# Where the image attention's short operations stand among the maxima of a two-layer cross-attention kernel

## The reference

```
# layer 0
q = x Wq;  out = softmax(q k_text) v_text + softmax(q k_img) v_img
x = out Wo + bo + x
# layer 1
probs_t = softmax(q k_t * scale);  text_out = probs_t v_t
attn_scores = q k_ip * scale                     # 4 image columns a head
qsem = l2norm(probs_t @ text);  ip_n = l2norm(ip)
fused = attn_scores + 0.5 * (qsem . ip_n)
probs_ip = softmax(fused) * spatial_mask
out = (text_out + probs_ip v_ip) W_out + b_out + x
```

## Time and profile before

| | |
|---|---|
| median of 3 runs | 2523.54 us (2521.98 to 2524.99) |
| the profiled execution's own time | 2525.83 us |
| its span | 2524.0 us |
| granted TensorE clock, mean | 0.996 |
| PE busy | 2444.6 us, 97% |
| DVE busy | 1642.0 us, 65% |
| ACT busy | 1228.2 us, 49% |
| POOL busy | 774.2 us, 31% |
| chain that ended last | PE 71%, DVE 17%, POOL 4% |

### The profile page before, as it was taken

How to read it: one execution, slowest core, us unless ns; L and a number is a source line. 1 busy time by engine, 2 the same in 40 slices (tenths; PEclk the granted TensorE clock), 3 DMA queues, 4 the chain that set the end, 5 groups by cost and what they waited for, 6 DMA issues and landing times.

```text
span 2524.0 us, 64056 instructions
## 1 busy us (share of the span) xinstructions
PE 2444.6 (97%) x26372; PEld 2117.5 (84%) x26372; DVE 1642.0 (65%) x3313; ACT 1228.2 (49%) x2251; POOL 774.2 (31%) x1030
## 2 busy tenths in 40 slices
PE   7899999999999999999999999999999999999998
PEld 6788888888888888888888888888888888888877
DVE  4456667666667666667656677566677666677665
ACT  3355444455444455444554454554454554444543
POOL 3133233233233232233232233332332332332322
PEclk9999999999999999999999999999999999999999
DMA  8865446674556754557655466645566655566620
GB/s 216 139 100 88 93 88 98 106 116 75 88 90 96 117 90 85 89 92 113 104 81 97 80 106 104 108 76 91 97 97 105 98 82 91 88 97 103 95 28 18
DMA packets 371689, 241.44 MB, mean 96 GB/s; under 512 B 131947, under 2 KB 365243, under 8 KB 371388
## 3 DMA queue, kind: packets, MB, share of 16 engines
q1 hardware_dynamic: 371398, 237.35, 56.6%
HBM read 171.35 MB, written 64.59 MB: 93 GB/s over the span
## 4 chain that ended last, share of the span: by engine, by line
PE 71%; DVE 17%; POOL 4%; DMA 2%; SPq 2%; issue 2%; ACT 1%; DVEq 0%; POOLq 0%; ACTq 0%
PE ST L832 7%; PE R L898 5%; PE R L763 5%; PE PN L871 5%; PE R L708 4%; DVE m L1090 4%; POOL w L1468 4%; PE R L776 4%; PE R L777 4%; PE R L709 4%; PE R L956 3%; DVE m L1094 3%; PE PN L916 3%; DVE w L992 3%; PE R L779 3%; PE R L711 3%
## 5 line engine op out<-in xcount | busy, mean ns | idle before, releaser
L1468 POOL TENSOR_TENSOR w<-w 128x448 f32<-128x448 f32 (+1 forms) x256 | 331.2, 1294 | 376.8 <-DVE w L989 358.0
L992 DVE SCALAR_TENSOR_TENSOR w<-p,pr 128x1344 f32<-128x1344 f32 x160 | 295.9, 1850 | 164.6 <-ACT pr L1352 151.0
L1324 ACT ACTIVATE p<-ST 128x1344 f32<-128x1344 f32 x260 | 335.5, 1290 | 99.0 <-PE ST L835 94.0
L989 DVE TENSOR_TENSOR rem<-R,kst 128x298 f32<-128x298 f32 (+2 forms) x180 | 89.4, 497 | 426.5 <-ACT kst L1207 426.3
L898 PE MATMUL R<-pr,Gh 128*128 128x448 f32 (+1 forms) x960 | 366.3, 382 | 0.0
L989 DVE TENSOR_TENSOR w<-R,w 128x448 f32<-128x448 f32 (+1 forms) x480 | 281.7, 620 | 69.4 <-PE R L903 59.2
L1400 POOL TENSOR_TENSOR kst<-rem,kst 128x298 bf16<-128x298 f32 (+2 forms) x180 | 148.0, 822 | 558.1 <-ACT kst L1207 305.2
L776 PE MATMUL R<-wvh,ch 128*128 128x320 f32 (+3 forms) x896 | 302.9, 338 | 0.0
L777 PE MATMUL R<-wvh,cl 128*128 128x320 f32 (+3 forms) x896 | 277.4, 310 | 0.0
L832 PE MATMUL ST<-Qs,Ks 100*128 100x112 bf16 (+1 forms) x3520 | 228.9, 214 | 8.2 <-ACT p L1324 2.7
L832 PEld LDWEIGHTS ST<-Qs,Ks 100*128 100x128 bf16 (+1 forms) x3520 | 187.9, 98 | 46.7 <-issue 13.4
(11 more groups left out here) (230 smaller groups left out, 5768.4 us busy)
## 6 DMA issues: line engine op xcount, KB each, us to landing
Ks<-k_split SPq DMA_DIRECT2D x384, 140.6 KB, 5.8
Ks<-k_split SPq DMA_DIRECT2D x384, 93.8 KB, 8.2
w<-in_ctxT SPq DMA_DIRECT2D x31, 750.0 KB, 10.1
k_split<-kst SPq DMA_DIRECT2D x64, 281.2 KB
k_split<-kst SPq DMA_DIRECT2D x64, 223.5 KB, 3.0
Qs<-q_split SPq DMA_DIRECT2D x64, 210.0 KB, 9.0
q_split<-qst SPq DMA_DIRECT2D x128, 84.0 KB, 2.3
Qs<-q_split SPq DMA_DIRECT2D x64, 140.0 KB, 9.1
```

The source lines that it names most:

```text
L989: return e.tensor_tensor(to, x, y, op)
L992: return e.scalar_tensor_tensor(out=to, in0=x, scalar=s, in1=y, op0=op0, op1=op1)
L1324: e.activation(to.rearrange("p (u q) -> p u q", u=3), st, ACT.Exp).then_inc(p_whole, 1)
L1468: e.tensor_tensor(first, first, w2[n % 2][0:ROWS[j], QW * j:QW * j + QW], ALU.add).then_inc(ns_added, 1)
```

## The change

```
-        o.add("fuse", b)
-        yield
-        o.add("ip_softmax", b)
-        yield
+        for step in ("root_inverse", "sem", "fuse", "fuse_max", "fuse_less", "ip_sum", "ip_inverse", "ip_softmax"):
+            o.add(step, b)
+            yield
...
-            if count[0] in (1, 2, 3, 5, 7, 9, 10):
+            if b + 1 == B:
+                take(last, (0, 1, 5, 3, 0, 1, 0, 1, 0, 1, 1)[count[0]])
+            elif count[0] in (1, 2, 3, 4, 5, 6, 7, 8, 9, 12, 13, 14, 16):
                 take(last, 1)
-            if count[0] in ((2, 3, 4, 6, 8, 12, 14, 16) if 0 < b < B - 1 else (2, 4, 6, 8, 11, 12, 14, 16)):
+            if count[0] in ((2, 3, 5, 6, 8, 11, 12, 14) if 0 < b < B - 1 else (2, 4, 6, 8, 11, 12, 14, 16)):
                 take(pieces, 1)
...
+                elif kind == "sem":
+                    b, = key
+                    f1 = fus[1]
+                    w.wait_ge(root_inverted, b + 1)
+                    tt(f1[:], num[:], sm[0][:].unsqueeze(2).to_broadcast([S, H, NIP]), ALU.mult).then_inc(num_read, 1)
...
-                elif kind == "fuse":
+                elif kind == "fuse_less":
                     b, = key
                     w.wait_ge(fus_less, b + 1)
                     e.activation(fus[0][:], fus[1][:], ACT.Exp).then_inc(ip_exp, 1)
```

More of the change, by code:

```diff
@@ L434, in stage_order @@
         take(rows0, 9)
-        for n in (17, 0, 0, 2, 5, 3, 0):
+        for n in (17, 0, 0, 0, 0, 0, 0, 0, 0, 2, 5, 3, 0):
             take(last, 1)
@@ L578, in xattn_two_layers @@
                              "ip_mm", "ip_added", "num_read"))
+        root_inverted, ip_max, ip_summed, ip_inverted = (
+            sem(n) for n in ("root_inverted", "ip_max", "ip_summed", "ip_inverted"))
         o_T, o_T_copied, o_mm, x_added, x1_T, x1_T_copied = (
@@ L1171, in vector @@
                         ALU.max).then_inc(d_bound, 1)
+                elif kind == "root_inverse":
+                    b, = key
+                    w.wait_ge(d_root, b + 1)
+                    e.reciprocal(sm[0][:], d2[:]).then_inc(root_inverted, 1)
+                elif kind == "sem":
+                    b, = key
+                    f1 = fus[1]
+                    w.wait_ge(root_inverted, b + 1)
+                    tt(f1[:], num[:], sm[0][:].unsqueeze(2).to_broadcast([S, H, NIP]), ALU.mult).then_inc(num_read, 1)
                 elif kind == "fuse":
@@ L1174, in vector @@
                     f0, f1 = fus
[L1175 to L1178, removed]
                     w.wait_ge(num_read, b + 1)
                     tt(f0[:], f1[:], sip[b % 2][:], ALU.add).then_inc(fused, 1)
+                elif kind == "fuse_max":
+                    b, = key
                     w.wait_ge(fused, b + 1)
-                    e.reduce_max(sm[1][:], f0[:], X).then_inc(dve_step, own.one())
-                    w.wait_ge(dve_step, own.n)
-                    tt(f1[:], f0[:], sm[1][:].unsqueeze(2).to_broadcast([S, H, NIP]), ALU.subtract).then_inc(fus_less, 1)
+                    e.reduce_max(sm[1][:], fus[0][:], X).then_inc(ip_max, 1)
+                elif kind == "fuse_less":
+                    b, = key
+                    f0, f1 = fus
+                    w.wait_ge(ip_max, b + 1)
+                    tt(f1[:], f0[:], sm[1][:].unsqueeze(2).to_broadcast([S, H, NIP]), ALU.subtract).then_inc(fus_less, 1)
+                elif kind == "ip_sum":
+                    b, = key
+                    w.wait_ge(ip_exp, b + 1)
+                    e.reduce_sum(sm[1][:], fus[0][:], X).then_inc(ip_summed, 1)
+                elif kind == "ip_inverse":
+                    b, = key
+                    w.wait_ge(ip_summed, b + 1)
+                    e.reciprocal(sm[2][:], sm[1][:]).then_inc(ip_inverted, 1)
                 elif kind == "ip_softmax":
@@ L1187, in vector @@
                     f0, f1 = fus
[L1188 to L1192, removed]
+                    w.wait_ge(ip_inverted, b + 1)
                     if b:
```

## The result

The changed kernel takes 2661.12 us (median of 4 runs, 2658.21 to 2662.26) against 2523.11 for the one before beside it (2521.98 to 2524.99): a ratio of 1.0538, 95% interval 1.0525 to 1.0550. It is 138 us slower, where 95 were forecast, and 11 us above the range. The profiled execution took 2662.1 us with a span of 2660.4.

What follows compares the result with a forecast made beforehand. The prediction took TensorE as the bound, busy nearly all the time with 71% of the chain. It added 30 x 2.4 + 29 x 0.8 = 95 us to the 2523.5 us median: 2619 us, range 2560 to 2650.

Steps and rivals of the forecast that it cites:

- The maxima, 2.4 us a turn: From the maxima's first product to the next scores: scores at 1274.7 against 1272.26, 2.4 us later in 30 turns.
- step 11: Product in the maxima on TensorE: forecast to start at 1263.4 against the old 1264.32, 0.9 us ahead.
- o_T: Transposition on TensorE behind step 14: waits for VectorE's addition to o_sum, TensorE idle for 1.15 us.
- The single waits of steps 9, 10 and 11: TensorE in the maxima waits for VectorE's reads, idle for 0.67, 0.54 and 1.15 us.
- rival 4: The clock falls behind the thinly filled steps 9 to 11: 90 us more, 2710 us; chance 0.04.
- bank wait: Value product behind o_T waits for ScalarE's copy, behind w4, to free its bank: 0.7 us idle, bound 0 to 0.7.
- The load of `xT`, 0.8 us: Behind the scores: load issued after the store, so the query product waits 0.8 us in 29 turns, bounds 0 to 1.3.
- VectorE's wait for ScalarE in place of the operations taken out: Ahead of the first Gram remainder: VectorE gains about 0.6 us, the rest of the saving turns into this wait.
- The short operation at 0.16 us: VectorE's short operation behind a read: taken at 0.16 us, bounds 0 to 0.27.
- Rival 1: Losses overlap: only the idle time of steps 9 to 11 counts, 39 us, giving 2563 us; chance 0.17.
- Rival 2: Faster: spread operations hide ahead of the reads, TensorE's idle 1.08 us a turn goes, 2491 us; chance 0.08.
- Rival 3: No effect: loss and gain cancel within 5 us; chance 0.03.

Runs made afterwards that it cites:

- e5_fill: Changed kernel plus idle matmuls, two behind step 9, three behind step 10, four ahead of the transposition at step 14: 2634.95 us.
- e2_xT_first: Changed kernel with the store of a finished element issued behind the load of xT instead of ahead of it: 2612.36 us.
- e11_recovered_bundled: Same as e9_recovered, but with the eight operations bundled as in the old kernel: 2567.52 us.
- e9_recovered: Changed kernel, eight operations still spread, with TensorE work moved forward, load ahead of store and the GpSimd-dependent copy put off to the next turn: 2565.91 us.
- e3_warm: Changed kernel plus idle matmuls of 128 columns, four behind step 9 and eight behind step 10: 2686.65 us.

## Why the prediction was partly wrong

The direction and the waits were right, the size was not: 95 us forecast, 138 measured. Two steps failed. The clock had been left out of the sum, with a chance of 0.04, and cost 23 to 26 us; and the new wait for `xT` was put at 0.8 us a turn and measured at 1.54, 21 us more in all. With either of the two as forecast, the time would have been within the range.

- *The maxima, 2.4 us a turn.* Right, for a turn whose clock holds: 26.5 us against 24.39, so 2.1. By the starts of rows, counted from the first product of the maxima, step 11 stands at 439.35 - 424.06 = 15.3 us (forecast 1263.4 - 1247.9 = 15.5), `o_T` at 21.3 (21.4), the value product at 22.4 (22.5), the next scores at 26.65 (26.8). The 2.4 was too much mainly because the old turn quoted is a short one: its maxima take 24.34 us, the mean of the 30, counted in the same way, is 24.53. The single waits of steps 9, 10 and 11, 0.43, 0.31 and 0.80 us (forecast 0.67, 0.54 and 1.15), of `o_T`, 1.02 (1.15), and of the value product, 0.57 (0.7), are each a little shorter than worked out.
- *The clock.* This is the first step that failed. The prediction had it as rival 4, set apart from the forecast, and argued against it that "no gap is longer than 1.2 us". The changed kernel has no longer gap in the maxima either, and its clock falls in twenty of 30 turns, around step 11, behind gaps of 0.45, 0.30 and 0.80 us. The rival's argument for itself, some 3.3 us with 1.1 us of work (from the start of the wait of step 9 to step 11 it is 439.35 - 436.53 = 2.8 us, with 1.3 of work, in the first turn above), was the one to weigh; what makes the clock hold in ten turns with the same waits, no run here shows. Its price, 3 us a turn, was near in the four turns at 0.66 or 0.67, whose maxima are 2.4 us longer than at full clock, and too high in the others, 0.8 us. On average it is 27.28 - 26.5 = 0.8 us, 23 us in all, and `e5_fill` gives back 26. What TensorE loses in a fall it partly doesn't wait for later, as in the twenty turns without a bank wait.
- *The load of `xT`, 0.8 us.* Right in kind, mis-sized, and this is the second step. The scores-to-issue distance was right, 452.09 - 450.71 = 1.38 against my 1.3. From issue to the product I took 2.5 us; it is 454.95 - 452.09 = 2.86 in the turn shown, 3.9 in the one at 1015.56, and 3.15 on average. The 2.5 lies between the least and the median of the earlier trace rows, measured where the loads had time to spare. For a load that is waited for in each turn, the mean with its late ones counts, and the loads behind a store landed later too (a mean of 3.02 us against 2.74 before). So the mean wait is above 1.3 us, the end of the bound that I had given. `e2_xT_first` removes it.
- *VectorE's wait for ScalarE in place of the operations taken out.* Right: 1.12 us ahead of the first remainder, and these waits grow from 16.0 us in 32 places before to 60.5 in 66.
- *The short operation at 0.16 us.* Right: 431.74 - 431.59 = 0.15. But it does not matter: bundled and spread orders take the same time as long as TensorE's order is one and the same (`e11_recovered_bundled`, `e9_recovered`).
- *Rivals 1 to 3.* Rival 1, the overlap, needs the later waits to vanish. The bank wait does so in twenty turns, but those for `o_sum` and `xT` are there 30 and 29 times. Rival 2, that spreading is itself a gain, is out by the result, and the gain on VectorE by itself by `e9_recovered` against `e11_recovered_bundled`. Rival 3, no effect, is out by the result too.

The sum as measured: 30 x 2.1 + 30 x 0.8 + 29 x 1.54 = 63 + 24 + 45 = 132 us of the 138; by the experiments, 49 for the load, 26 for the clock, 18 for the copy in front of GpSimd, and 43 for the cover moved away from steps 9 to 11 and the wait for `o_sum`, whose shares I did not take apart.

## What to carry over

An instruction moved off a place costs what it covered there, whether or not it was waited for: work of TensorE between two waits is cover and keeps the clock, so look at the busy time of the whole stretch and not at its longest gap alone. At the new place price each thing that now stands behind it in an in-order queue, a load behind a store or an exponential behind a copy that waits for a third engine. When a short gap can't be filled with useful work, a few idle matmuls may be worth more than they cost, if they fit in it. And a load that a move puts on the path is to be priced by its mean time to landing, late ones included.

## What the runs showed of the hardware

- In the changed kernel the granted clock is 0.66 to 0.80 of full speed on average over 8.5 us of the maxima in twenty turns, where TensorE never idles for more than 1.1 us at a time in the maxima, and 1.00 in ten others with the same waits. Of its levels, 2.4 and 1.2 GHz, the lower one shows in a 320-column matmul of 0.47 us instead of 0.31. In the turn shown it is back at 0.95 on average in the 7.5 us that follow.
- Two, three and four idle matmuls kept it at 1.00 in all 30 maxima (`e5_fill`). With four and eight at the first two places alone (`e3_warm`) it held there, but fell in ten turns behind the next two waits, of 1.03 and 0.57 us.
- Such a 128-column matmul on float32, two instructions in the trace, took 0.22 us of TensorE's time.
- The load into `xT` took 2.4/2.6/8.8 us (least, median, most of the whole span) to landing in the kernel before, and 2.7/2.8/8.9 in the changed one, where it is issued right behind a store. In 29 turns of each it took over 3 us in four and in ten of them; in `e2_xT_first`, where it stands ahead of the store, in none.
